# Weighted neighbours summed on TensorE in 32 by 32 tiles instead of on GpSimd and VectorE

## The reference, cut to what matters

```python
for i, dil in enumerate((1, 2, 4, 8)):
    q, k, v = (qkv[:, 0, i], qkv[:, 1, i], qkv[:, 2, i])
    attn = einsum('bhdn,bhdkn->bhnk', qh, unfold3x3(k, dil)) * scale   # 9 scores a pixel
    attn = softmax(attn, axis=-1)
    o = einsum('bhnk,bhdkn->bnhd', attn, unfold3x3(v, dil))            # weighted sum of 9 neighbours
x = x + concatenate([outs[i] * gate[:, i] for i in range(4)], axis=1)
x = x + second_attention(group_norm(x))                                # per image
```

## Time and profile before

| | us |
|---|---|
| median of three runs | 90.8 |
| lowest, highest | 89.75, 91.09 |
| the profiled execution, first to last instruction (span) | 88.6 |

### The profile page before, as it was taken

The page is one execution under the profiler, slowest core; times in us unless marked ns, Lnnn a source line. Parts: engine busy times, 40 slices in busy tenths (PEclk is TensorE's granted clock), DMA queues, the critical chain, the costliest instruction groups (busy, mean ns, idle before and its releaser), DMA issues.

```text
span 88.6 us, 2254 instructions
## 1 busy us (share of the span) xinstructions
PE 71.5 (81%) x896; PEld 55.5 (63%) x896; DVE 74.1 (84%) x193; ACT 33.9 (38%) x104; POOL 45.6 (52%) x82
## 2 busy tenths in 40 slices
PE   0299997999967899295998799995998098999970
PEld 0299784576425797193988677794876054766840
DVE  1278399999999969999699888999999959875990
ACT  4496699063650000000018333040695036367220
POOL 7404585068000199793999998699992000600000
PEclk9999999999999999999999999999999858999999
DMA  1992013000000000000000000000000000003145
GB/s 24 326 360 62 0 33 64 0 0 7 0 0 4 4 7 0 0 0 0 4 7 0 0 0 0 0 0 7 0 0 7 0 0 4 0 0 118 43 145 174
DMA packets 3019, 3.11 MB, mean 35 GB/s; under 512 B 320, under 2 KB 2752, under 8 KB 3008
## 3 DMA queue, kind: packets, MB, share of 16 engines
q1 hardware_dynamic: 2576, 2.69, 9.6%
q10 hardware_dynamic: 432, 0.26, 1.3%
HBM read 1.91 MB, written 1.05 MB: 33 GB/s over the span
## 4 chain that ended last, share of the span: by engine, by line
DVE 45%; PE 28%; POOL 12%; issue 5%; ACT 4%; DMA 4%; DVEq 0%; ACTq 0%
PE ps L818 27%; DVE qk L615 22%; DVE pv L665 10%; POOL pv L368 6%; POOL acc L368 6%; DMA xt<-x_dram 4%; DVE acc L677 3%; DVE pv L677 3%; DVE ssum L632 1%; PE ps L954 1%; DVE x L710 1%; ACT pT L445 1%; DVE acc L665 1%; DVE x L684 1%; DVE smax L622 1%
## 5 line engine op out<-in xcount | busy, mean ns | idle before, releaser
L818 PE MATMUL ps<-prob,sel 128*128 128x180 f32 (+6 forms) x120 | 18.7, 309 | 4.8 <-DVE pv L665 3.6
L818 PEld LDWEIGHTS ps<-prob,sel 128*128 128x128 f32 x120 | 17.0, 190 | 6.9 <-DVE pv L665 5.1
L615 DVE TENSOR_TENSOR qk<-q,k 128x128 f32<-128x128 f32 (+7 forms) x36 | 21.1, 650 | 0.1
L665 DVE TENSOR_TENSOR pv<-ps,v 128x128 f32<-128x128 f32 (+7 forms) x32 | 17.1, 568 | 2.4 <-PE ps L818 2.0
L368 POOL TENSOR_TENSOR pv<-pv 128x240 f32<-128x240 f32 (+3 forms) x24 | 16.2, 682 | 2.0 <-DVE pv L665 1.8
L818 PE MATMUL ps<-xn,wp 128*32 128x256 f32 (+1 forms) x208 | 16.4, 382 | 0.1
L368 POOL TENSOR_TENSOR acc<-acc,pv 128x256 f32<-128x256 f32 (+4 forms) x20 | 13.2, 664 | 0.5
L333 POOL TENSOR_TENSOR rstd<-gvar,mhalf 128x2 f32<-128x2 f32 (+1 forms) x6 | 4.9, 824 | 15.4 <-DVE gvar L563 15.3
L818 PEld LDWEIGHTS ps<-xn,wp 128*32 128x32 f32 (+1 forms) x208 | 9.8, 116 | 4.4 <-ACT xn L452 0.6
L423 ACT ACTIVATE expd<-shifted 128x576 f32<-128x576 f32 x2 | 1.4, 683 | 21.3 <-DVE shifted L625 21.3
L818 PE MATMUL ps<-xt 128*128 128x128 f32 x28 | 5.9, 382 | 3.9 <-DMA xt<-x_dram 3.9
(11 more groups left out here) (81 smaller groups left out, 104.2 us busy)
## 6 DMA issues: line engine op xcount, KB each, us to landing
xt<-x_dram SPq DMA_DIRECT2D x4, 256.0 KB, 3.5
out_dram<-x SPq DMA_DIRECT2D x8, 128.0 KB, 1.8
wp<-wpack_dram SPq DMA_DIRECT2D x1, 325.0 KB, 5.3
sel<-selc_dram SPq DMA_DIRECT2D x4, 64.0 KB, 3.9
cs<-consts_dram ACTq DMA_DIRECT2D x1, 130.0 KB, 3.5
cs<-consts_dram ACTq DMA_DIRECT2D x2, 64.0 KB, 2.6
```

The lines of the kernel that those rows point to most:

```text
L615: last = nc.vector.tensor_tensor(o, a, b, ALU.mult)
L665: last = nc.vector.tensor_tensor(o, a, b, ALU.mult)
L818: return nc.tensor.matmul(o, w, m, start=start, stop=stop)
```

## The change

GpSimd sums only units 0 and 1 of phase 1. All of phase 0, and units 2 and 3 of phase 1, are added on TensorE: for each slot of nine, each unit s and each image slot j, one matmul with a 32 by 32 identity (rows 32j, columns 32s), accumulating in PSUM over the slots, each over its rectangle. It does the adding and the restoring in one. `restore` is gone, and `keep_clock(2, 1)`, `keep_clock(3, 1)` with it. The second phase's products go into the `qk` tiles, which are free by then, so that phase 0's `pv` stays readable; VectorE no longer waits for `added` there. All four images of a phase are finished together (the four increments of `restored` come with the last slot of unit 3). Phase 0's sum stands in two parts: units 0 to 2 ahead of `spread(1,0,0)`, unit 3 where `restore(0)` was.

```diff
-POOL_SUMS = (ND, 2)
+POOL_SUMS = 2
-RSQRT_AFTER = ((1, 0, 4), (1, 1, 0))
+RSQRT_AFTER = ((0, 4), (1, 0))
-        acc = sb("acc", [P, PHASES, ND, N])
+        acc = sb("acc", [P, POOL_SUMS, N])
+        products = (pv, qk)
+        def neighbours(s):
+            return [(3 * ci + ri, *valid_rows(s, ri), *columns(DIL[s], ci)[:2])
+                    for ci in CENTRE_FIRST for ri in CENTRE_FIRST]
@@ gpsimd
-            for ph in range(PHASES):
-                for s in range(POOL_SUMS[ph]):
+            for s in range(POOL_SUMS):
...
@@ vector, multiply_pv
-                if ph and chunk == 0:
-                    dve.wait_ge(added, ADDS * (s + 1))
-                    o = view(pv[s], (3 * ci + ri) * N + r0 * W + c0, [[dri * N + dr * W, n], [W, rows], [1, nc_]])
-                    if ci == 1 and n == 1:
-                        o = view(acc, (ph * ND + s) * N, [[W, rows], [1, nc_]])
+                    o = view(products[ph][s], (3 * ci + ri) * N + r0 * W + c0,
+                             [[dri * N + dr * W, n], [W, rows], [1, nc_]])
@@ vector, order
             multiply_pv(1, 3, 0)
-            add_neighbours(1, 2)
             for i in range(1, 3):
                 multiply_pv(1, 3, i)
-            add_neighbours(1, 3)
             attention_shift(0)
@@ tensor
+            def sum_neighbours(ph, units):
+                parts = []
+                for s in units:
+                    if ph and s < POOL_SUMS:
+                        pe.wait_ge(added, ADDS * (s + 1))
+                        parts.append([(acc, s * N, 0, H, 0, W)])
+                    else:
+                        parts.append([(products[ph][s], slot * N, r0, r1, c0, c1)
+                                      for slot, r0, r1, c0, c1 in neighbours(s)])
+                pe.wait_ge(pv_ready, 12 * ph + 3 * (max(units) + 1))
+                if ph == 0:
+                    pe.wait_ge(shift_ready, PHASES)
+                for n in range(KK):
+                    for s, part in zip(units, parts):
+                        if n >= len(part):
+                            continue
+                        t, offset, r0, r1, c0, c1 = part[n]
+                        dims = [[W, r1 - r0], [1, c1 - c0]]
+                        for j in range(SLOTS):
+                            rows = slice(32 * j, 32 * j + 32)
+                            last = mm(view(ps, 512 * (BANK[2 * ph] + j) + r0 * W + c0, dims, 32 * s, 32),
+                                      ident[rows, rows], view(t, offset + r0 * W + c0, dims, 32 * j, 32),
+                                      start=(n == 0), stop=(n == len(part) - 1))
+                            if n == KK - 1 and s == ND - 1:
+                                last.then_inc(restored, 1)
@@ tensor, order
                 spread(0, 3, i)
-            keep_clock(2, 1)
-            keep_clock(3, 1)
+            sum_neighbours(0, (0, 1, 2))
             for i in range(2):
                 spread(1, 0, i)
-            restore(0)
+            sum_neighbours(0, (3,))
             spread(1, 0, 2)
             spread(1, 1, 0)
             group_stats(0)
-            restore(1)
...
             attention(1)
-            restore(2)
-            restore(3)
+            sum_neighbours(1, (0, 1, 2, 3))
             fuse(0, 0)
```

More of the change, by code:

```diff
@@ L237, in build @@
         added = sem("added")
-        dve_added = sem("dve_added")
         restored = sem("restored")
@@ L272, in of_phase, with operands @@
             return slice(ph, B, PHASES)
-        def operands(ph, s, n, target, slot):
+        products = (pv, qk)
+        def neighbours(s):
+            return [(3 * ci + ri, *valid_rows(s, ri), *columns(DIL[s], ci)[:2])
+                    for ci in CENTRE_FIRST for ri in CENTRE_FIRST]
+        def operands(s, n, target, slot):
             ci, ri = divmod(slot, 3)
@@ L281, in rect @@
                 return t.rearrange("p (r c) -> p r c", c=W)[:, r0:r1, c0:c1]
-            o = rect(acc[:, ph, s, :] if target == 4 else pv[s][:, target, :])
-            a = rect(pv[s][:, 4, :]) if n == 0 and PAD[s] else o
-            return o, a, rect(pv[s][:, slot, :])
+            product = products[PHASES - 1][s]
+            o = rect(acc[:, s, :] if target == 4 else product[:, target, :])
+            a = rect(product[:, 4, :]) if n == 0 else o
+            return o, a, rect(product[:, slot, :])
         block = ctx.enter_context(nc.Block())
@@ L356, in _ @@
             nc.gpsimd.tensor_tensor(gate[:], gsel[:], grec[:], ALU.mult).then_inc(gate_ready, 1)
-            base = 0
-            for ph in range(PHASES):
-                for s in range(POOL_SUMS[ph]):
[L361 to L372, removed]
+            for s in range(POOL_SUMS):
+                for n, (target, slot, after) in enumerate(additions(s)):
+                    chunk = 12 * (PHASES - 1) + 3 * s + ADD_NEEDS[n]
+                    if n == 0 or ADD_NEEDS[n] > ADD_NEEDS[n - 1]:
+                        pool.wait_ge(pv_ready, chunk)
+                    if after is not None:
+                        pool.wait_ge(added, ADDS * s + after + 1)
+                    o, a, b = operands(s, n, target, slot)
+                    nc.gpsimd.tensor_tensor(o, a, b, ALU.add).then_inc(added, 1)
+                    if (s, n) in RSQRT_AFTER:
+                        g = RSQRT_AFTER.index((s, n))
+                        rsqrt(PHASES + g, group(g))
             for g in range(len(RSQRT_AFTER), GROUPS):
@@ L666, in multiply_pv @@
                 last.then_inc(pv_ready, 1)
[L668 to L677, removed]
             def first_residual(g):
@@ L818, in mm, with keep_clock @@
                 return nc.tensor.matmul(o, w, m, start=start, stop=stop)
-            def keep_clock(n, shifted=0):
-                if shifted:
-                    pe.wait_ge(shift_ready, shifted)
+            def keep_clock(n):
                 for _ in range(n):
@@ L918, in spread @@
                 last.then_inc(spread_ready, 1)
[L920 to L926, removed]
-                if ph == 0:
[L928 to L935, removed]
+            def sum_neighbours(ph, units):
[8 more added lines that the diff above has]
+                pe.wait_ge(pv_ready, 12 * ph + 3 * (max(units) + 1))
+                if ph == 0:
+                    pe.wait_ge(shift_ready, PHASES)
[12 more added lines that the diff above has]
+                                last.then_inc(restored, 1)
             def group_stats(g):
```

## The result

The changed kernel takes 93.25 us (median of four runs, 93.06 to 93.83), the kernel before 90.94 us beside it. The ratio is 1.038, with a 95% interval of 1.029 to 1.047: slower. The profiled execution has a span of 91.2 us, where before had 88.6.

A forecast was written before the change was run, and what follows sets the result against it. Neither VectorE (84% busy) nor TensorE (81%) alone was taken as the bound. Successive gains carried through the chain made `first_residual(3)` 2.25 us earlier, with nothing changed behind it: 88.6 us, range 87.2 to 92.5 us.

The forecast's parts named there:

- Part 1: Phase 1's products of units 2 and 3 on VectorE: 3.4 us less without GpSimd's phase 0 additions beside them.
- The rival of a gain that doesn't come through: TensorE's spreads hold phase 0, so VectorE's relief gives some 1.5 us instead of 3.4: 90.5 us; chance 0.1.
- Part 2: Phase 0's first sum on TensorE: all tiles together, 3.7 us, so `spread(1,0,0)` starts 1.7 us earlier, not 3.4.
- partial overlap or a cost per instruction: Phase 0's first sum takes about 5 us, not 3.7: 89.8 us, or 91.6 with 60 cycles each; chance 0.2.
- Part 3: From `spread(1,0,0)` through phase 1's products to `attention(1)`: `multiply_pv(1,0,2)` starts 1.4 us earlier, at 53.85 us.
- Part 4: Phase 1's sum to `first_residual(3)`: sum 2.7 us at full clock, `first_residual(2)` 1.8 us earlier, total 2.25 us earlier.
- My rival: Low attention-stage work still halves the clock, now on phase 1's sum: up to 2.7 us more, 91.3 us; chance 0.08.
- The four-tile rival: Only four tiles run together in the sums: first part 9.9 us, time 97.3 us; four tiles or worse, chance 0.15.

The follow-up runs named there:

- the kernel whose clock was kept: The changed kernel with six idle 128 by 128 matmuls behind phase 1's sum; 91.19 us, 1.010 of the kernel before.
- The shifted kernel: The changed kernel with six idle matmuls behind phase 1's sum, plus 24 tiny matmuls (96 TensorE instructions) at the very start; 91.08 us, 1.015 of the kernel before.

## Why the prediction was wrong, point by point

- **Part 1, GpSimd's silence.** Right in mechanism and price: 1.48 + 1.56 us where I said about 2.9, against 6.3. But I let all 3.4 us through, and 2.97 came (1.92 by the profiles, 1.05 hidden by the later start): VectorE then waited for `spread` 0.94 us at 41.15, where before it had waited for 0.47 us. The rival of a gain that doesn't come through was real, with 0.4 us.
- **Part 2, the rate.** The failed step in the sum of costs: the first sum priced at its longest tile, 3.7 us, with nothing for its instructions. All tiles do run together: in the first sum twelve instructions start within 0.08 us, and their successors from 0.24 us on. I took at most 0.014 us an instruction from 32 short matmuls in 0.46 us, a burst that is over before a steady rate shows, and used it to set aside a cost per instruction. Measured is an average of 0.019: 4.17 us for the first sum, not 3.7, and 3.1 at best for the last, not 2.7. The Trainium skill's 0.025 us (TensorEngine Tiling (Array Packing), Instruction Overhead), by which the first sum was 5.4 us, was too high by about a third, but its warning pointed the right way, and my row was no measure of it. The rival *partial overlap or a cost per instruction* had that part. That its 89.8 to 91.6 us holds the 91.2 us of the kernel whose clock was kept is partly luck: those 91.2 us also hold the gap of 0.8 us, which the rival did not have.
- **Part 3, through phase 1's products.** 6.12 us from the spread to `multiply_pv(1,0,2)`, where I had 5.75: the second sum 1.88 instead of 1.7, the two spreads 2.71 instead of 2.6. It kept its distance from there to `attention(1)`, as forecast. The 1.7 us that the place ahead of `spread(1,0,0)` should cost were 2.3.
- **Part 4, phase 1's sum.** 4.05 us from first matmul to residual instead of 2.95. The shifted kernel, whose sum has no gap, takes 3.22 us. So 0.27 is the sum's own length, and 0.83 the gap without a wait, which the prediction's price had nothing for.
- **The clock.** I counted the restores' return to full clock as a gain and took nothing for a new stretch. The half clock didn't go away, it moved behind the sum, since TensorE now has its idle time there, waiting for `fuse(0,0)`'s operand for 1.6 us. It cost 1.2 us in the profile, and 2.1 us of median came back with idle matmuls. It is the largest single term of the miss of 4.65 us in the median, and my sum had it at nothing. My rival had the right mechanism with the wrong place, and only 0.08.
- **The base.** My sum was made against one execution, with its full clock at about 9 us and its restores at half clock. In executions with a granted clock of 1.0 the kernel before has spans from 87.6 us: 1.0 us of what I meant to save was never lost in such runs.
- **The four-tile rival** fell: no sum comes near 9.9 us.

What stays open: why the instructions stop for 0.4 to 0.8 us at one place in a long run of them (position decides in the one shift that was tried; the cause was only argued), and whether the first sum's 0.5 us too much is a rate or an end.

## What to carry to other kernels

Work that is moved into many small matmuls can be paid by the instruction, even where the tiles overlap: take both the longest tile and the count of instructions times a rate, and measure the rate over some hundred of them, not over a burst. Taking additions off GpSimd can be worth something to VectorE too (3.4 us here), but the gain is spent if the work goes to the engine that holds the end next. And before a difference of 1 or 2% is read as the change's, look where TensorE was idle and what clock it was granted behind that: six matmuls that compute nothing gave back more than half of the loss.

## What the runs showed of the hardware

- Twelve 32 by 32 tiles of float32 matmuls run at once (twelve starts within 0.08 us, the next from 0.24 us on). Sums of 160 to 288 such instructions, over rectangles that accumulate in PSUM, averaged 0.0191 to 0.0199 us for a MATMUL with its weight load, though single ones start 0.007 us apart; sums of 72 and 96 averaged 0.022 to 0.026.
- Some long runs of TensorE instructions (160 to 288) have gaps of 0.4 to 0.8 us with no wait. One moved to another sum when 96 instructions were put ahead.
- Ten VectorE products of two SBUF tiles took 3.0 us alone and 6.5 us beside GpSimd's additions.
- By the pace of its matmuls, TensorE came to its full clock at 7 to 14 us from one execution to the next, in profiles of kernels whose beginnings are the same, though the view of the granted clock gives 1.00 from the start. Between the two executions compared here that is most of 1.05 us of span. With work on a constant tile from 1 us on, it came at 4.7 to 5.5 us in three profiles.
- Behind a stretch of 2.7 us in which TensorE was busy for 1.06 us, the granted clock was 0.50 for over 3 us; with six idle matmuls in that stretch it stayed at 1.00.
